# Moving one part's preparation into another: three token groups, half of a weight merge, the last low parts and an output product in a five-part transformer kernel

## The reference

```python
h = concat(patches(x) @ W + b, table[x_txt])                # [32, 192, 256]
h = h + attention(layernorm(h))                             # causal, 256 channels
h = h + ternary_ffn(layernorm(h))                           # 1024 hidden, GELU, rms norm before each product
# recurrent part, 512 channels, one step per token
xz = ln(h) @ Win.T ; xi, z = split(xz)
lam = exp(-8 * softplus(omega) * sigmoid(xi @ Wl.T + bl)) ; v = xi @ Wv.T + bv
hs_t = lam_t * (hs - 2 v_t (v_t . hs) / (v_t . v_t)) + (1 - lam_t) * xi_t
h = h + (silu(z) * hs) @ Wout.T
# experts: 8, two picked per token, swiglu, for the rows that the reference weights
h = h + experts(ln(h))
```

## Time and profile before

| | us |
|---|---|
| median of 3 runs (lowest, highest) | 1030.51 (1027.21, 1032.54) |
| the profiled execution's own time | 1034.37 |
| its span, first to last instruction | 1032.6 |
| busy: PE, PEld, DVE, ACT, POOL | 934.5, 837.2, 786.5, 592.1, 545.4 |
| mean granted clock of TensorE, as a share of full | 0.957 |

### The profile page before, as it was taken

How to read it: one execution, slowest core, us unless ns; L and a number is a source line. 1 busy time by engine, 2 the same in 40 slices (tenths; PEclk the granted TensorE clock), 3 DMA queues, 4 the chain that set the end, 5 groups by cost and what they waited for, 6 DMA issues and landing times. The chain is left out here.

```text
span 1032.6 us, 19334 instructions
## 1 busy us (share of the span) xinstructions
PE 934.5 (91%) x5800; PEld 837.2 (81%) x5800; DVE 786.5 (76%) x2393; ACT 592.1 (57%) x1174; POOL 545.4 (53%) x652
## 2 busy tenths in 40 slices
PE   2689999999999999869799999999999999963998
PEld 2689999999999999765587888887888888852887
DVE  3678777777777777652588898988999999972676
ACT  1346666666666666634566676666666666621442
POOL 4156676767676765445244454545555554422573
PEclk9889999999999999988989999999999999975999
DMA  5001111111111140012999999999999999982310
GB/s 208 21 26 42 42 42 41 41 41 41 41 41 41 44 171 22 17 27 76 102 128 142 149 159 139 157 141 152 151 156 150 146 163 141 135 96 94 123 62 21
DMA packets 134814, 96.32 MB, mean 93 GB/s; under 512 B 11208, under 2 KB 129104, under 8 KB 134096
## 3 DMA queue, kind: packets, MB, share of 16 engines
q1 hardware_dynamic: 133200, 91.20, 58.3%
q0 software_dynamic: 1536, 4.20, 1.4%
HBM read 31.92 MB, written 13.11 MB: 44 GB/s over the span
## 5 line engine op out<-in xcount | busy, mean ns | idle before, releaser
L315 POOL TENSOR_TENSOR gelu_lo<-gelu_out,gelu_hi 128x384 fp32r<-128x384 f32 x128 | 151.0, 1208 | 29.9 <-DVE gelu_hi L529 29.4
L944 POOL TENSOR_TENSOR B_decayed_u<-B_scan_in 128x512 f32<-128x512 f32 x48 | 62.0, 1292 | 97.1 <-DMA B_scan_in<-B_stage 88.5
L708 PE MATMUL psA<-ternary_down,gelu_hi 128*128 128x256 f32 x384 | 96.9, 291 | 6.9 <-POOL gelu_lo L315 6.3
L652 PE MATMUL psA<-x2T_hi,ternary_up 128*128 128x384 f32 x256 | 94.7, 370 | 3.4 <-DVE residual L642 3.2
L708 PE MATMUL psA<-ternary_down,gelu_lo 128*128 128x256 f32 x384 | 93.3, 282 | 0.0
L652 PE MATMUL psA<-x2T_lo,ternary_up 128*128 128x384 f32 x256 | 88.5, 346 | 0.0
L932 POOL TENSOR_TENSOR B_y<-B_scan_in,B_states 128x512 f32<-128x512 f32 x48 | 61.9, 1289 | 41.9 <-ACT B_states L1003 41.9
L1192 PEld LDWEIGHTS psB<-B_partial_dots,B_minus_same_batch 128*128 128x128 f32 x384 | 66.4, 194 | 21.8 <-DVE B_partial_dots L1076 10.6
L1180 PE MATMUL psB<-Win_hi,B_x_hi 128*128 128x512 f32 x192 | 83.6, 435 | 0.0
L708 PEld LDWEIGHTS psA<-ternary_down,gelu_hi 128*128 128x128 f32 x384 | 72.2, 188 | 11.4 <-POOL gelu_lo L315 10.2
L1092 DVE SCALAR_TENSOR_TENSOR psB<-B_decayed_u,psB 128x128 f32<-128x128 f32 x192 | 68.0, 354 | 12.7 <-PE psB L1192 12.2
(11 more groups left out here) (251 smaller groups left out, 3329.5 us busy)
## 6 DMA issues: line engine op xcount, KB each, us to landing
B_scan_in<-B_stage SPq DMA_DIRECT2D x192, 256.0 KB, 8.1
patches<-in_patches SPq DMA_DIRECT2D x16, 384.0 KB
B_residual<-layer_out SPq DMA_DIRECT2D x48, 128.0 KB, 5.2
out_dram<-B_residual SPq DMA_DIRECT2D x48, 128.0 KB, 5.0
C_raw<-in_experts SPq DMA_DIRECT2D x8, 768.0 KB, 4.4
layer_out<-residual SPq DMA_DIRECT2D x32, 128.0 KB, 1.8
layer_out<-residual SPq DMA_DIRECT2D x32, 64.0 KB, 2.0
raw_Wl<-in_upT SPq DMA_DIRECT2D x1, 1024.0 KB, 9.1
```

The costliest lines, as they stand in the source:

```text
L315: nc.gpsimd.tensor_tensor(act_l[:, k, :], act[:, k % DEEP, :], act_h[:, k, :].bitcast(F32), ALU.subtract).then_inc(s["ffn_lo"], 1)
L652: last = nc.tensor.matmul(out, a, b, start=(n == 0), stop=(n == len(terms) - 1))
L708: last = nc.tensor.matmul(ps[:, 6 + k // 2, (k % 2) * D:(k % 2 + 1) * D], x[:, c, k * P:(k + 1) * P], dn_w[:, c, :], start=(c == 0 and x i ...
L944: nc.gpsimd.tensor_tensor(lu[:, j % 2], ring[:, j % R_RING, :, LAM, :], ring[:, j % R_RING, :, U, :], ALU.mult).then_inc(s["lu"], 1)
```

## The change

It touches all three parts.

First part: in the last group TensorE turns Win before the up products (`turn_win`), ScalarE copies it out, and the eight products of the first two merges (`fold`, those with Wl) are made behind up.2, up.4, up.6 and down.2. Of the eight low parts of this group VectorE makes those of k = 1, 3, 5, 7. Its adds are written as scalar_tensor_tensor. Wout is no longer loaded here. One PSUM tensor serves both the first and the recurrent part.

Recurrent part: it begins with the two merges with Wv; Wout is loaded here. Three rounds are added to the preparation (tiles 48 to 50), whose rows are tokens 0 to 127 of sequences 0, 1 and 2, loaded from the output when tile 31 is stored. Their high and low parts go where the experts' part reads them. The experts' small inputs and two raw experts are loaded at turn 30 (`TT - 18`), expert 0's weights are split at turns 36 (ScalarE) and 38 (GpSimd). The fourth group (tokens 128 to 191 of sequences 0 and 1) is loaded from the output up to its last four tokens, and these are copied from the residual. Behind each dot product of the last three tiles TensorE makes six transposes whose result isn't used. The output products of tiles 44 and 45 are parted: three matmuls at the old place, nine behind the first dot product of the next turn. The waits for the last stores move to the end of the experts' part, the clearing of its semaphores to SyncE at the head of the recurrent part.

Experts' part: expert 0's gate_up is done in two halves of 256 columns (groups 0 and 1, then 2 and 3), with the routing weights' transposes and the fourth group's norm, transposes and split between. Each group of 128 rows is stored when its last sum is made, the fourth in two transfers.

```diff
+        order_last.insert(0, ("turn_win", 0))
+        for m, behind in enumerate((("up", 2), ("up", 4), ("up", 6), ("down", 2), ("down", 2), ("down", 2), ("down", 2), ("down", 2))):
+            at = order_last.index(behind) + 1
+            while order_last[at][0] == "fold":
+                at += 1
+            order_last.insert(at, ("fold", m))
...
+        last_lo_vector = (1, 3, 5, 7)
...
-                    for a, b in ((W.raw_in, io["WinT"]), (W.raw_l, io["WlT"]), (W.raw_v, io["WvT"]), (W.raw_out, io["WoutT"])):
+                    for a, b in ((W.raw_in, io["WinT"]), (W.raw_l, io["WlT"]), (W.raw_v, io["WvT"])):
...
+                if kind == "turn_win":
+                    for half_nat in range(2):
+                        sc.wait_ge(s["nat_ps"], half_nat + 1)
+                        nc.scalar.activation(W.nat[:, 2 * half_nat:2 * half_nat + 2, :].rearrange("p a b -> p (a b)"),
+                                             ps[:, (4, 2)[half_nat], :], ACT.Copy).then_inc(s["nat_ready"], 1)
...
+                if kind == "gelu" and isinstance(n, int) and n == G - 1 and k in last_lo_vector:
...
+                    nc.vector.scalar_tensor_tensor(out=act_l[:, k, :], in0=act[:, k % DEEP, :], scalar=1.0,
+                                                   in1=act_h[:, k, :].bitcast(F32), op0=ALU.mult,
+                                                   op1=ALU.subtract).then_inc(s["ffn_lo_v"], 1)
+                if kind == "add" and isinstance(n, int) and n == G - 1:
+                    v.wait_ge(s["sq_done"], FC * n + k + 1)
+                    if k > 1:
+                        v.wait_ge(s["sqsum_done"], (FC - 1) * n + k - 1)
+                    nc.vector.scalar_tensor_tensor(out=sqsum[:], in0=sqsum[:], scalar=1.0, in1=sq[:, k % DEEP, :],
+                                                   op0=ALU.mult, op1=ALU.add).then_inc(s["sqsum_done"], 1)
+                elif kind == "add":
...
+                if kind == "turn_win":
+                    pe.wait_ge(s["raw_in"], 48)
+                    pe.wait_ge(s["h1_done"], G)
+                    for m in range(IC):
+                        for c in range(DC):
+                            last = nc.tensor.transpose(ps[:, (4, 2)[m // 2], (m % 2) * D + c * P:(m % 2) * D + (c + 1) * P],
+                                                       W.raw_in[:, c, m * P:(m + 1) * P], ident[:])
+                        if m % 2:
+                            last.then_inc(s["nat_ps"], 1)
+                if kind == "fold":
+                    pe.wait_ge(s["nat_ready"], 2)
+                    group, m = k // IC, k % IC
+                    nc.tensor.matmul(ps[:, group, :], W.nat[:, m, group * P:(group + 1) * P], W.raw_l[:, m, :],
+                                     start=(m == 0), stop=(m == IC - 1))
...
+            sp.dma_start(raw_out[:].rearrange("p a b -> p (a b)"), io["WoutT"]).then_inc(s["wout_in"], 16)
+            for sem_ in E.s.values():
+                sp.sem_clear(sem_)
             for i in range(FIRST, LAST):
+                if i == TT - 18:
+                    for a, b in ((E.b_up, io["up_bias"]), (E.b_dn, io["down_bias"])):
+                        sp.dma_start(a[:], b).then_inc(E.s["const_in"], 16)
+
+                    for a, b in ((E.picked, io["picked"]), (E.weights, io["routing"])):
+                        for q, lo, hi, q_in, lo_in in ((0, 0, P, 0, 0), (2, 0, P, 3, 0), (1, 0, 64, 1, 64), (1, 64, P, 2, 0),
+                                                       (3, 0, 64, 1, 0), (3, 64, P, 2, 64)):
+                            sp.dma_start(a[lo:hi, q, :], b[lo_in:lo_in + hi - lo, q_in, :]).then_inc(E.s["const_in"], 16)
+                    sp.wait_ge(s["w_lo"], 3)
+                    sp.wait_ge(s["m_ps"], 2)
+                    for e in range(2):
+                        sp.dma_start(E.raw[e], io["experts"][e]).then_inc(E.s["raw_in%d" % e], 16)
+                if i + 9 in range(TT, TT + 3):
+                    q = i + 9 - TT
+                    for j in range(28, 32):
+                        wait_stored(sp, j)
+                    sp.dma_start(E.acc[:, q, :], io["out"][q, 0:P, :]).then_inc(res_in[(TT + q) % 8], 16)
+                if i == TT + 1:
+                    for j in range(TT - 5, TT - 1):
+                        wait_stored(sp, j)
+                    for b in range(2):
+                        sp.dma_start(E.acc[b * (P // 2):b * (P // 2) + 60, 3, :],
+                                     io["out"][b, P:T - 4, :]).then_inc(E.s["h_in"], 16)
...
+                    if j == TT - 1:
+                        for b in range(2):
+                            sp.dma_start(E.acc[b * (P // 2) + 60:(b + 1) * (P // 2), 3, :],
+                                         res[4 * b:4 * b + 4, j % R_RES, :]).then_inc(E.s["h_in"], 16)
                     sp.dma_start(io["out"][:, 4 * j:4 * j + 4, :], res[:, j % R_RES, :]).then_inc(stored[j % 4], 16)
...
-            for j in range(TT - 4, TT):
-                wait_stored(sp, j)
...
-                if has(i + 5):
+                if has_x(i + 5):
...
+                if i == TT - 10:
+                    pool.wait_ge(E.s["w_hi"], 1)
+                    nc.gpsimd.tensor_tensor(E.w_l[:], E.raw[0], E.w_h[:].bitcast(F32), ALU.subtract).then_inc(E.s["w_lo"], 1)
...
+            merged(0)
+            merged(1)
...
+                if i == TT - 12:
+                    sc.wait_ge(E.s["raw_in0"], 16)
+                    nc.scalar.activation(E.w_h[:], E.raw[0], ACT.Copy).then_inc(E.s["w_hi"], 1)
+                if has_x(i + 4):
                     j = i + 4
...
-                    merged(0)
                     sc.wait_ge(s["rows_in"], 16)
                     sc.wait_ge(s["m_lo"], 1)
                     prefill_l(0)
-                    merged(1)
-                    nc.scalar.activation(out_h[:], W.raw_out[:], ACT.Copy).then_inc(s["w_hi"], 1)
                     merged(2)
                     merged(3)
+                    sc.wait_ge(s["wout_in"], 16)
+                    nc.scalar.activation(out_h[:], raw_out[:], ACT.Copy).then_inc(s["w_hi"], 1)
...
+            merged(0)
+            merged(1)
...
-            for m in range(IC):
-                for c in range(DC):
-                    last = nc.tensor.transpose(ps[:, STATE + m // 2, (m % 2) * D + c * P:(m % 2) * D + (c + 1) * P],
-                                               W.raw_in[:, c, m * P:(m + 1) * P], ident[:])
-                if m % 2:
-                    last.then_inc(s["nat_ps"], 1)
-            pe.wait_ge(s["nat_ready"], 2)
-
...
-            merge(0)
+            merge(2)
+            merge(3)
...
+                if i >= TT - 3:
+
+                    pe.wait_ge(s["u"], TT)
+                    for _ in range(6):
+                        nc.tensor.transpose(ps[:, bank("v", TT - 1), 0:P], ident[:], ident[:])
+
+            def wout(j, first, stop):
...
+                for n in range(first, stop):
+                    last = nc.tensor.matmul(ps[:, OUT, 0:D], *terms[n], start=(n == 0), stop=(n == len(terms) - 1))
+                if stop == len(terms):
+                    last.then_inc(s["wout"], 1)
...
+            parted = (TT - 4, TT - 3)
             for i in range(FIRST, LAST):
                 step(i, 0)
+                if i - 2 in parted:
+                    wout(i - 2, 3, 3 * IC)
...
-                    for n in range(1, 4):
-                        merge(n)
                     pe.wait_ge(s["m_lo"], 2)
...
+                    wait(pe, s["x_lo"], min(i + 5, TT + 3))
+                    wout(j, 0, 3 if j in parted else 3 * IC)
...
-            sp.dma_start(acc[:], rows).then_inc(s["h_in"], 16)
-            for a, b in ((picked, io["picked"]), (weights, io["routing"]), (b_up, io["up_bias"]), (b_dn, io["down_bias"])):
-                sp.dma_start(a[:], b).then_inc(s["const_in"], 16)
-            for e in range(E_N):
-                if e >= 2:
-                    sp.wait_ge(s["w_lo"], e - 1)
-                sp.dma_start(raw[:, e % 2, :], io["experts"][e]).then_inc(raw_in[e % 2], 16)
+            for e in range(2, E_N):
+                sp.wait_ge(s["w_lo"], e - 1)
+                sp.dma_start(raw[e % 2], io["experts"][e]).then_inc(raw_in[e % 2], 16)
+            for q in range(4):
+                sp.wait_ge(E.stored[q], 16 * (T // 16))
+            for q in range(3):
+                sp.wait_ge(s["acc"], MQ * (E_N - 1) + q + 1)
+                sp.dma_start(io["out"][q, 0:P, :], acc[:, q, :]).then_inc(s["stored"], 16)
             sp.wait_ge(s["acc"], MQ * E_N)
-            sp.dma_start(rows, acc[:]).then_inc(s["stored"], 16)
-            sp.wait_ge(s["stored"], 16)
+            for b in range(2):
+                sp.dma_start(io["out"][b, P:T, :],
+                             acc[b * (P // 2):(b + 1) * (P // 2), 3, :]).then_inc(s["stored"], 16)
+            sp.wait_ge(s["stored"], 80)
 
...
             split(1)
+            sc.wait_ge(s["shift"], 1)
```

(35 more changed lines are left out.)

193 lines of the change are left out of this document (100 added, 93 removed).

## The result

The changed kernel takes 1003.36 us (median of 4 runs, 1001.35 to 1004.80), the kernel before, in 4 runs beside it, 1029.40 (1027.21 to 1032.54): a ratio of 0.9743 with a 95% interval of 0.9711 to 0.9776. It is 26.0 us faster; forecast were 18.3, and 1003.36 lies just under the range's low end of 1004. The profiled execution has a span of 1001.5 us, 31.1 less than before's 1032.6; before's profiled execution (1034.37) lies 5 us above the median of its runs, the changed kernel's (1003.52) on its own. So some 5 of the 31.1 us are chance. The ratios leave out the few executions that took over 1.5% longer than the fastest of their kernel, such as one of e5's twelve, of 1517.88 us at a granted clock of 0.554.

A forecast was written before the change was run, and what follows sets the result against it. In the loop, ring transfers (8.1 us, DMA never free) and VectorE both bind. Terms -2.5 - 5.6 + 4 + 1 - 0.5 - 2.2 - 11.8 - 0.7 = -18.3 us, off the median 1030.51: 1012.2 us, range 1004 to 1021.

The forecast's parts named there:

- Term 1: End of the first part: shared low parts, with transposes and folds moved in, save 2.5 us (0 to 4.5).
- Term 2: Head of the recurrent part: first ring issued sooner, GpSimd's root then being late instead of TensorE; -5.6 us (-3.5 to -8.8).
- Term 3: Experts' transfers in the loop: SyncE's issues and bulk loads delay the ring of tile 32; +4 us (1.5 to 7).
- Terms 4 and 5: Expert 0's split in the loop, +1 us (0 to 2); end of the loop, -0.5 us (-3 to +4).
- Term 6: Last output product: fillers keep TensorE's clock full; -2.2 us (0 to -3).
- Term 7: Head of the experts' part: less work between last residual and second expert's product; -11.8 us (-8 to -14).
- 8 end: End of the kernel: the last 512 KB store becomes two of 64 KB; -0.7 us.
- slower: Rival, loop: tiles go from 8.4 to 9.4 us, 1042 us if all 48 do; chance 0.05.
- None like it elsewhere: Sign, loop: VectorE waits once for a ring, 2.5 to 4 us near tile 32, and nowhere else so.
- The -1 that I derived from the rule: End of the first part: if VectorE's low parts wait for GpSimd's, the gain of 2.5 us shrinks to about 1.
- More than summed: Rival: full clock through the experts' head and GpSimd's end of the first part halved; 1004 us, chance 0.06.

The follow-up runs named there:

- e5: Kernel before, padded so that B_stage (ring source) lies on a multiple of 256 bytes and B_scan_in (target) stays 224 above one: 1034.07 us, ratio 0.9986.
- e2: Changed kernel with a 224-byte pad, so that B_stage and B_scan_in lie 224 bytes above a multiple of 256: 1021.67 us, ratio 0.9888.
- e1: Kernel before with a 32-byte pad a partition, so that B_stage and B_scan_in lie on multiples of 256 bytes: 1019.59 us, ratio 0.9874.
- e6: Kernel before, padded so that B_scan_in (ring target) lies on a multiple of 256 bytes and B_stage stays 224 above one: 1019.28 us, ratio 0.9867.
- e4: Changed kernel with the experts' fourteen small loads spread over turns 2 to 15 and the 768 KB loads in turns 30 and 32: 995.16 us, ratio 0.9632.
- e13: Changed kernel with the fourteen small loads spread over turns 2 to 15, both 768 KB loads still in turn 30: 999.39 us, ratio 0.9692.
- e14: Changed kernel with the fourteen small loads still in turn 30, the 768 KB loads moved to turns 33 and 35: 999.44 us, ratio 0.9687.
- e8: e4 with expert 0's split cut into three pieces each on ScalarE (turns 36 to 38) and GpSimd (turns 39 to 41): 996.34 us, ratio 0.9639.
- e3: Changed kernel without the six filler transposes behind each of the last twelve dot products: 1006.49 us, ratio 0.9738.
- e12: Changed kernel with the output products of tiles 44 and 45 whole, as before the change: 1006.87 us, ratio 0.9725.

## Why the prediction was wrong, point by point

The stretches are read between the same events of both traces: the earlier trace rows and their counterparts above.

| | forecast | measured, from the traces |
|---|---|---|
| 1 end of first part | -2.5 | -1.6 (16.8 to 15.3) |
| 2 last residual to first ring issue | -5.6 | -6.0 (31.8 to 25.8) |
| 3 + 4 + 5 loop, without placement | +4.5 | +7.7 (e2: 419.7 to 427.4; e1 to after: 405.3 to 413.0) |
| placement, in the loop | no term | -14.4 (e1), -14.5 (e6), -14.4 (e2 to after) |
| 6 last product to last residual | -2.2 | -2.1 (10.1 to 8.1) |
| 7 to the second expert's product | -11.8 | -14.2 (28.45 to 14.22) |
| 8 end | -0.7 | -0.5 (67.3 to 66.8) |

They add up to -31.1, the difference of the spans; two stretches of 0.2 us, one each way, are left out. The medians differ by 5 us less, and which stretch that belongs to isn't known.

**The step that failed** is one that the sum had no term for. "What bounds the kernel now" took the ring's 8.1 us and the DMA share above 1 as given, and the loop's pace as something that the change could only disturb ("Nothing in the trace says why tempo changes"). The packet records did say it: 73 ns for 512 bytes, with the target at 224 over a multiple of 256. What no row told is that the address sets this price. The change moved the target to a multiple, packets fell to 62.6 ns, and the ring stopped holding up VectorE and `B_stage`. Shown by e1, e2 and e6 from both sides; e5 excludes the source. The slower tempo was the ring arriving late: tiles of 9.0 to 10.1 us, of which the kernel before has nine among tiles 2 to 46, are gone in e1 and e6 (8.9 at most there), and it went the other way than the rival "slower" feared. With the placement undone (e2) the change is worth 11.5 us, or 14.2 by spans. That makes 1017.9 us, inside the range of 1004 to 1021 and 6 above the forecast; some 3 of these are terms 3 to 5.

**Term 3** was mis-sized: forecast +4, measured +8 (e4's loop) where the ring has slack, and more where it has none (a wait of 9.8 us in e2). The mechanism was right, a late SyncE and a late ring behind bulk data, with one wait at tile 32. The sizes were not: sixteen issues last 9.2 us (753.75 to 762.99) instead of 7.2, 0.58 each instead of 0.45, and I let the two delays overlap, where e13 and e14 show that they add up. "None like it elsewhere" held. The Trainium skill, DMA: Bandwidth & Descriptors, section Queues, rings and completion order, has each DMA engine take descriptors in ring order, by which a later ring stands behind an earlier bulk load; e13's ring, begun on time and awaited for 2.4 us, agrees.

**Terms 4 and 5.** Tiles of 9.4 and 9.3 us stand where ScalarE's and GpSimd's long pieces are, nearly 1 us above 8.55 each, in place of +1 in all; e8 confirms the place. GpSimd's piece took 3.51 us, as forecast 3.5, but the wait for a dot behind it is 0.43 us, not about 1. VectorE's wait of 1.60 us in the last tile is gone, as said.

**Term 1** came to -1.6. Sharing brought 2.7 ("2 to 3 us earlier") and the rest took 1.2 ("about 1 us goes back"); the text had both and still put down -2.5. On the lock, VectorE's rows of the changed kernel:

```profile
444.37 0.36 DVE L548 CAST gelu_hi<-gelu_out 128x384 fp32r<-128x384 f32 x1
444.94 1.09 DVE L548 CAST gelu_hi<-gelu_out 128x384 fp32r<-128x384 f32 x1 [0.21 <-ACT gelu_out L398]
446.06 0.56 DVE L554 SCALAR_TENSOR_TENSOR gelu_lo<-gelu_out,gelu_hi 128x384 fp32r<-128x384 f32 x1
...
450.42 0.86 DVE L554 SCALAR_TENSOR_TENSOR gelu_lo<-gelu_out,gelu_hi 128x384 fp32r<-128x384 f32 x1 [0.65 <-ACT gelu_hi L407]
```

The cast that meets GpSimd's low part (444.81 to 445.81) takes 1.09 us instead of 0.36. VectorE's own low part, with two inputs in SBUF, takes 0.86 instead of 0.56 where it meets one of GpSimd's (449.86 to 450.87). In both the trace agrees with the rule of the Trainium skill, SBUF — State Buffer, section Who interferes with whom, by which a VectorE instruction with two SBUF inputs, and a cast if it is in a mode with two ports (no row shows the mode), can wait for one of GpSimd that reads SBUF. But exclusion does not undo the sharing: a low part on VectorE takes 0.56 us against GpSimd's 1.0 to 1.3, so even one after the other is shorter. The -1 that I derived from the rule had left that out.

**Term 2** held within 0.4 us, and so did the first ring issue (485.83; forecast near 485.5). The reason held too: ScalarE waits for GpSimd's root.

```profile
481.27 0.69 ACT L1145 ACTIVATE B_stage<-psAB,B_v_scale 128x512 f32<-128x512 f32 x1 [3.57 <-POOL B_v_scale L1031]
```

**Term 6** held, but not for the reason given alone. In e1, which has neither fillers nor parts, that stretch is 8.8 us; in e3 (placement, no fillers) and in e2 (fillers, no placement) it is 8.9. Of the gain of 2.1 either without the other brings 1.2 to 1.3, and e12 shows nothing for the parts (8.1).

**Term 7** was -14.2, just beyond its low bound of -14: 14.2 us lie between the last residual and the second expert's product instead of 16 to 17. By the chain: 2.9 us to the first half product (3.2 in the text), 4.6 and 3.1 for the halves (8.04), 1.8 between them (3.5), 1.9 for the bias. The turning between the halves was read too dear.

The rival "More than summed" named 1004 us, with 0.06, and the time came out there by coincidence: it rests on a full clock in the experts' head and on GpSimd's share of the first part's end halved. Term 1 fell short, and the clock fell during the first half product, which took 4.55 us where the second took 3.13:

```profile
924.00:928.00 4.00, 4.00 (x25) 3.94 (x25) 2.00 (x18) 1.18 (x2) 1.55 (x5) 0.67 0.59 197
```

## What to carry to other kernels

Before forecasting an edit to on-chip memory, list the start addresses of the tiles that a saturating DMA writes to, before and after: 32 bytes of padding a partition made the kernel before 1.3% faster, as much as all the work of the change. When a stage has a DMA share near 1, divide by packets and ask what one costs; the pace that varied for no visible reason was, here, a ring with next to no slack. And spread small issues over idle turns of the issuing queue: fourteen loads in a row cost 3 to 4 us, one a turn nothing that the tiles of turns 2 to 15 show (8.5 to 8.6 us).

## What the runs showed of the hardware

A transfer within SBUF in packets of 512 bytes costs by where it is written. At offsets 0, 32, 64, 192 and 224 over a multiple of 256 a packet took 62.9, 70.7, 66.9, 70.8 and 73.2 ns; the source's offset changed nothing (73.1 against 73.2). The Trainium skill, DMA: Bandwidth & Descriptors, section How a descriptor splits into AXI transactions, describes the reading side: a transaction begins at the multiple of 256 below the start, and the bytes before the start cost beats of 32 bytes all the same. An estimate by that rule is 16 beats for 512 bytes from a multiple, 17 from 32, 18 from 64, 22 from 192 and 23 from 224. The runs show no such cost of reading here, and their order of offsets on the writing side is another: 32 costs as much as 192. Why is open; I did not try 128, other packet sizes or transfers from DRAM.
